# Cross-channel attention, 16 batches: X and G loaded a second time, and turned by 32x32 transposes on VectorE instead of on TensorE

## The reference

```python
def xca(q, k, v):
    attn = softmax(einsum('bhni,bhnj->bhij', q, k) * scale, axis=-1)
    return einsum('bhnd,bhde->bhne', v, attn)
res_p2r = xca(heads(rgb, wq_rgb), heads(geo, wk_point), heads(geo, wv_point)) @ proj_p2r.T
res_r2p = xca(heads(geo, wq_point), heads(rgb, wk_rgb), heads(rgb, wv_rgb)) @ proj_r2p.T
out = transpose(rgb + res_p2r) + transpose(geo + res_r2p)
```

## Time and profile before

| | |
|---|---|
| median of the runs | 145.45 us (145.23, 145.67, 145.45) |
| profiled execution, span of the trace | 144.7 us |
| TensorE busy | 135.4 us, 94% |
| VectorE busy | 99.1 us, 68% |
| ScalarE busy | 92.6 us, 64% |
| GpSimd busy | 2.0 us, 1% |
| DMA | 25.80 MB, 178 GB/s over the span |

### The profile page before, as it was taken

One profiled execution on the slowest core, in us unless ns is written; L12 is line 12 of the kernel. 1 busy time (PEld: TensorE's weight loads), 2 busy tenths in 40 slices (PEclk: granted clock), 3 DMA queues, 4 the chain that ended last, 5 costly groups with the idle time before them and its releaser, 6 DMA issues. The chain is left out here.

```text
span 144.7 us, 3130 instructions
## 1 busy us (share of the span) xinstructions
PE 135.4 (94%) x968; PEld 123.4 (85%) x968; DVE 99.1 (68%) x245; ACT 92.6 (64%) x207; POOL 2.0 (1%) x11
## 2 busy tenths in 40 slices
PE   7599889999999999999999999999999999997871
PEld 7399778999999998999999998989999998986560
DVE  0125797678686977777786878777785969777740
ACT  3125948675766767785876767686867677582821
POOL 5000000000000000000000000000000000000000
PEclk9959999999999999999999999999999999999998
DMA  4999243431919467482828475583927730303033
GB/s 132 246 418 417 96 140 150 147 147 31 348 61 248 191 183 249 142 289 60 296 86 263 172 239 196 165 270 89 310 53 245 317 147 0 145 0 150 2 147 145
DMA packets 7642, 25.80 MB, mean 178 GB/s; under 512 B 849, under 2 KB 977, under 8 KB 7633
## 3 DMA queue, kind: packets, MB, share of 16 engines
q1 hardware_dynamic: 7632, 25.69, 52.2%
HBM read 17.30 MB, written 8.39 MB: 178 GB/s over the span
## 5 line engine op out<-in xcount | busy, mean ns | idle before, releaser
L383 DVE COPY gt<-gt_ps 128x512 f32<-128x512 f32 x32 | 22.1, 691 | 18.1 <-PE gt_ps L228 18.1
L238 PE MATMUL gu_ps<-gt,xt 128*128 128x128 f32 x256 | 34.5, 281 | 0.0
L238 PEld LDWEIGHTS gu_ps<-gt,xt 128*128 128x128 f32 x256 | 33.2, 198 | 1.2
L372 ACT COPY out_sb<-out_ps 128x512 f32<-128x512 f32 x32 | 17.7, 587 | 18.0 <-DMA out_dram<-out_sb 11.0
L387 DVE TENSOR_TENSOR x_lo<-x_raw,x_hi 128x1024 fp32r<-128x1024 f32 x16 | 19.6, 1226 | 4.1 <-ACT x_hi L327 4.1
L318 ACT COPY xt<-xt_ps 128x512 f32<-128x512 f32 x32 | 18.9, 589 | 5.0 <-PE xt_ps L228 4.9
L354 ACT ACTIVATE expd<-scores,min_neg 128x128 f32<-128x128 f32 x32 | 12.6, 395 | 12.8 <-DVE min_neg L427 12.8
L228 PE MATMUL xt_ps<-ident,x_raw 128*128 128x128 f32 x128 | 19.3, 273 | 1.1 <-DMA x_raw<-in_x_dram 1.1
L228 PE MATMUL gt_ps<-ident,g_raw 128*128 128x128 f32 x128 | 19.8, 278 | 0.6 <-DMA g_raw<-in_ctx_dram 0.6
L387 DVE TENSOR_TENSOR g_lo<-g_raw,g_hi 128x1024 fp32r<-128x1024 f32 x16 | 19.5, 1216 | 0.0
L228 PEld LDWEIGHTS xt_ps<-ident,x_raw 128*128 128x128 f32 x128 | 15.4, 142 | 3.2 <-DMA x_raw<-in_x_dram 1.3
(11 more groups left out here) (51 smaller groups left out, 193.1 us busy)
## 6 DMA issues: line engine op xcount, KB each, us to landing
x_raw<-in_x_dram SPq DMA_DIRECT2D x15, 512.0 KB, 3.5
g_raw<-in_ctx_dram SPq DMA_DIRECT2D x15, 512.0 KB, 5.3
out_dram<-out_sb SPq DMA_DIRECT2D x15, 512.0 KB, 5.9
x_raw<-in_x_dram SPq DMA_DIRECT2D x2, 256.0 KB, 3.8
g_raw<-in_ctx_dram SPq DMA_DIRECT2D x2, 256.0 KB, 4.4
out_dram<-out_sb SPq DMA_DIRECT2D x2, 256.0 KB, 2.0
w_sb<-in_weights_dram SPq DMA_DIRECT2D x1, 384.0 KB, 7.1
w_sb<-in_weights_dram SPq DMA_DIRECT2D x1, 128.0 KB, 5.0
```

The source lines that it names most:

```text
L238: last = nc.tensor.matmul(gram_ps, xt[:, cols], gt[:, cols], start=(t == 0), stop=(t == TILES - 1))
L372: nc.scalar.copy(out_sb[:, slot % OUT_SLOTS, cols], out_ps[:, cols]).then_inc(half_copied, 1)
L383: nc.vector.tensor_copy(gt[:, cols], gt_ps[:, cols]).then_inc(gt_copied, 1)
```

## The change

- TensorE's 256 blocks turned against the identity are gone, with the 64 PSUM copies behind them. The PSUM that they took holds separate banks for gram, u/v, scores, exponentials, y and T.
- X and G are each loaded twice: once as before (`load_plain`, raw blocks for the split and the output), and once by `load_turned` into `xz` and `gz`. A "quad" is 32 partitions. The load of quad q brings pixels 256q to 256q+255 of all 128 channels to partitions 32q to 32q+31: channel 32a+k goes to partition 32q+k, column block a. That is one DMA per quad and tensor, of 1 KB rows: 128 rows for batches 0 and 1, 256 rows for a pair of batches after them. The quads go in the order 0, 2, 1, 3, all from SyncE. Two pairs of batches are held.
- VectorE turns 32x32 blocks with its own transpose (`turn_half`), four instructions of 128x512 in a step, from SBUF to SBUF. The pixels end up in another order within the sum, the same for X and G.
- The low parts of X and G (128x1024 each) move from VectorE to GpSimd, and wait there for the output stage of four batches before.
- The stages are one step deeper: VectorE turns batch i while TensorE makes gram i-1, small i-2, last i-3. T's matmuls are at the end of the small stage. ScalarE copies the second output half in the next step, and splits X of a batch before the gram's high part.
- The exponentials and the T sum stay in PSUM, the product with the reciprocal is one instruction instead of two, the output has four slots, and 56 warm-up matmuls stand in place of 24.
- The separate versions of the last steps (u/v copied by VectorE, T's high part made there) are gone, and the loops are written out.

```diff
-WARM = 24
+WARM = 56
-OUT_SLOTS = 2
+OUT_SLOTS = 4
+        def load_turned(eng, src, dst, done, first, count, quads):
+            pair, at = first // 2 % PAIRS, first % 2
+            for q in quads:
+                into = dst[q * QUAD:(q + 1) * QUAD, pair, at:at + count, :]
+                eng.dma_start(into.rearrange("p e (a m) -> p (e a) m", a=QUADS),
+                              src[q][:, QUADS * first:QUADS * (first + count), :]).then_inc(done, 16)
...
+            for b in range(B):
+                split_lo(b, x_raw, x_hi, x_lo, x_hi_ready)
+                split_lo(b, g_raw, g_hi, g_lo, g_hi_ready)
...
+            load_turned(sp, x_turn, xz, xz_first, 0, 1, (0, 2, 1, 3))
+            load_turned(sp, g_turn, gz, gz_first, 0, 1, (0, 2, 1, 3))
             sp.dma_start(w_sb[:, WQR:WKR + 1, :], weights[:, WQR:WKR + 1, :]).then_inc(wu_loaded, 16)
+            load_turned(sp, x_turn, xz, xz_loaded[0], 1, 1, (0, 2, 1, 3))
+            load_turned(sp, g_turn, gz, gz_loaded[0], 1, 1, (0, 2, 1, 3))
+            load_plain(0)
             sp.dma_start(w_sb[:, WKP:, :], weights[:, WKP:, :]).then_inc(w_loaded, 16)
+            load_turned(sp, x_turn, xz, xz_loaded[1], 2, 2, (0, 2, 1, 3))
+            load_turned(sp, g_turn, gz, gz_loaded[1], 2, 2, (0, 2, 1, 3))
+            for b in range(1, SLOTS):
+                load_plain(b)
+            for i in range(2, B + 4):
+                if i % 2 == 0 and i + 2 < B:
+                    sp.wait_ge(xt_turned, 2 * i)
+                    sp.wait_ge(gt_turned, 2 * i)
+                    load_turned(sp, x_turn, xz, xz_loaded[(i + 2) // 2 % PAIRS], i + 2, 2, (0, 2, 1, 3))
+                    load_turned(sp, g_turn, gz, gz_loaded[(i + 2) // 2 % PAIRS], i + 2, 2, (0, 2, 1, 3))
+                if 0 <= i - 4 < B - 1:
+                    store(i - 4)
+                if i >= 3 and i + 1 < B:
+                    sp.wait_ge(lo_ready, 2 * (i - 3) + 2)
+                    load_plain(i + 1)
...
+                if out_on:
+                    evacuate(e, 1)
...
+                if gram_on:
+                    split_hi(g, x_raw, x_loaded, x_hi, x_hi_ready)
...
+                if last_on:
+                    evacuate(l, 0)
                 if gram_on:
+                    act.wait_ge(gram_done, g + 1)
...
                     nc.scalar.copy(gram_hi[:, :], gram_ps).then_inc(gram_hi_ready, 1)
+                    split_hi(g, g_raw, g_loaded, g_hi, g_hi_ready)
...
+                blocks = src[:, pair, b % 2, :].rearrange("p (a j i) -> p j a i", a=QUADS, i=QUAD)
+                first = half * TILES // 2
                 cols = slice(half * HALF, (half + 1) * HALF)
+                nc.vector.transpose(dst[:, b % 2, cols].rearrange("p (j a k) -> p j a k", a=QUADS, k=QUAD),
+                                    blocks[:, first:first + TILES // 2, :, :]).then_inc(turned, 1)
```

More of the change, by code:

```diff
@@ L187, in _ @@
[L187 to L191, removed]
+                sp.dma_start(out[b], out_sb[:, b % OUT_SLOTS, :]).then_inc(out_stored[b % OUT_SLOTS], 16)
@@ L215, in _, with gram_half @@
                 nc.tensor.matmul(out_ps[:, 0:P], warm[:, :], warm[:, :], start=True, stop=True)
[L216 to L225, removed]
+            def gram_half(b, half):
+                pe.wait_ge(xt_turned, 2 * b + 1 + half)
+                pe.wait_ge(gt_turned, 2 * b + 1 + half)
+                if half == 0 and b >= 1:
+                    pe.wait_ge(gram_lo_ready, b)
@@ L226, in turn @@
                 for t in range(half * TILES // 2, (half + 1) * TILES // 2):
                     cols = slice(t * TILE, (t + 1) * TILE)
[L228 to L238, removed]
+                    last = nc.tensor.matmul(gram_ps, xt[:, b % 2, cols], gt[:, b % 2, cols], start=(t == 0),
+                                            stop=(t == TILES - 1))
@@ L239, in gram_half, with last_parts @@
                 if half == 1:
                     last.then_inc(gram_done, 1)
-            def last_half(b, slot, half, b_min):
+            def last_parts(b, half, first, end):
+                slot = b % SLOTS
                 cols = slice(half * HALF, (half + 1) * HALF)
-                if b_min >= 1:
-                    pe.wait_ge(half_copied, 2 * b - 1 + half)
                 parts = [(t_hi, 0, x_hi), (t_hi, 0, x_lo), (t_hi, 1, g_hi), (t_hi, 1, g_lo), (t_lo, 0, x_hi), (t_lo, 1, g_hi)]
-                for n, (w, which, moving) in enumerate(parts):
+                if first == 0 and b >= 1:
+                    pe.wait_ge(half_copied, 2 * (b - 1) + 1 + half)
+                for n in range(first, end):
+                    w, which, moving = parts[n]
@@ L248, in last_half @@
                     if half == 0 and n == 4:
                         pe.wait_ge(t_lo_ready, b + 1)
[L250 to L259, removed]
+                    last = nc.tensor.matmul(out_ps[:, cols], w[:, which, :], moving[:, slot, cols], start=(n == 0),
+                                            stop=(n == len(parts) - 1))
@@ L260, in step @@
+                if end == len(parts):
+                    last.then_inc(half_done, 1)
+            for i in range(1, B + 3):
+                g, s, l = i - 1, i - 2, i - 3
+                gram_on, small_on, last_on = g < B, 0 <= s < B, 0 <= l < B
                 if small_on:
-                    pe.wait_ge(gram_lo_ready, i)
-                    if i_min == 1:
+                    pe.wait_ge(gram_lo_ready, s + 1)
+                    if s == 0:
                         pe.wait_ge(wu_lo_ready, 1)
@@ L306, in step @@
                 if last_on:
-                    last_half(i - 2, before, 1, i_min - 2)
-            steps(pe, step, 0, B + 1)
+                    last_parts(l, 1, 2, 6)
+                if small_on:
+                    pe.wait_ge(y_copied, s + 1)
+                    if s >= 1:
+                        pe.wait_ge(t_lo_ready, s)
+                    nc.tensor.matmul(t_ps[:, 0:P], y_sb[:, 1, :], w_sb[:, PR, :], start=True, stop=True)
+                    nc.tensor.matmul(t_ps[:, P:2 * P], y_sb[:, 0, :], w_sb[:, PP, :], start=True,
+                                     stop=True).then_inc(t_done, 1)
@@ L374, in _, with split_hi, evacuate @@
-            steps(act, step, 0, B + 1)
+            def split_hi(b, raw, loaded, hi, hi_ready):
+                slot = b % SLOTS
+                act.wait_ge(loaded[slot], 16 * (b // SLOTS) + 16)
+                if b >= SLOTS:
+                    act.wait_ge(half_done, 2 * (b - SLOTS) + 2)
+                nc.scalar.copy(hi[:, slot, :], raw[:, slot, :]).then_inc(hi_ready, 1)
+            def evacuate(b, half):
+                act.wait_ge(half_done, 2 * b + 1 + half)
+                if half == 0 and b >= OUT_SLOTS:
+                    act.wait_ge(out_stored[b % OUT_SLOTS], 16 * (b // OUT_SLOTS))
+                cols = slice(half * HALF, (half + 1) * HALF)
+                nc.scalar.copy(out_sb[:, b % OUT_SLOTS, cols], out_ps[:, cols]).then_inc(half_copied, 1)
@@ new lines, in turn_half @@
+            def turn_half(b, half, src, first_loaded, loaded, dst, turned):
+                pair = b // 2 % PAIRS
+                if b == 0:
+                    dve.wait_ge(first_loaded, 64)
+                elif b == 1:
+                    dve.wait_ge(loaded[0], 64)
+                else:
+                    dve.wait_ge(loaded[pair], 64 * (b // 2 // PAIRS) + 64)
+                if b >= 2:
+                    dve.wait_ge(gram_done, b - 1)
+                blocks = src[:, pair, b % 2, :].rearrange("p (a j i) -> p j a i", a=QUADS, i=QUAD)
+                first = half * TILES // 2
+                cols = slice(half * HALF, (half + 1) * HALF)
+                nc.vector.transpose(dst[:, b % 2, cols].rearrange("p (j a k) -> p j a k", a=QUADS, k=QUAD),
+                                    blocks[:, first:first + TILES // 2, :, :]).then_inc(turned, 1)
```

302 lines of the change are left out of this document (122 added, 180 removed).

## The result

The changed kernel takes **164.94 us** (median of 4 runs, 161.84 to 170.02), the kernel before beside it 145.56 (4 runs, 145.23 to 146.64): ratio 1.1164, 95% interval 1.1078 to 1.1251. It was forecast at 139 us, 6 us quicker than before; it is 19 us slower by the medians, 17 by the ratio, so the sign was wrong, and the median lies 0.94 us above the end of the range.

What follows compares the result with a forecast made beforehand. DMA was taken as the bound: 16.78 MB turned at 280 GB/s (59.9 us) and 18.35 MB at 415 (44.2), from 2.2 us, reach 106.3; with 5.1, 12.9, 6.6 and 7.7 after, 138.6, plus 0.75: 139 us, range 121 to 164.

Steps and rivals of the forecast that it cites:

- Bounds of a turned load's rate: DMA of the second, turned loads: between 187 and 417 GB/s, taken as 280, so 16.78 MB take 59.9 us.
- half-rate rival: DMA: turned loads run at half the full rate, 208 GB/s, taking 80.7 us, 160 us in all; chance 0.36.
- X: Time when the last turned pair (batches 14, 15) has landed in the DMA queue, put at 106.3 us.
- tail: After the last turned pair lands: VectorE's turning 5.1 us, two full steps 12.9, then 6.6 and 7.7 us.
- VectorE's turning among its other work: First term after the last turned pair has landed: VectorE turns it within its step's work, 5.1 us.
- I take the queue as never empty: DMA queue until the last turned pair lands: always filled, since each load is issued two steps ahead of use.
- TensorE, 6.43 us a step: TensorE's step without turning falls from 8.09 by 1.66 to 6.43 us, 26.6 us over 16 steps.
- VectorE, 0.69 us a transpose: Four 512-column transposes a step on VectorE at 0.69 us, 2.8 us, together 5.1 us a step.
- the rival of double cost: VectorE's transposes take 1.38 us each, a step 7.9 us, 145 us in all, no change; VectorE-bound chance 0.06.
- GpSimd, 4.8 us a step, hidden: Two low parts of 1024 columns a step on GpSimd, 3.2 to 6.4 us, middle 4.8, needed two steps later.
- SyncE, 2.3 to 2.7 us of issue a step: SyncE issues 7 DMAs a step in 2.3 to 2.7 us, 4.1 if 256 rows cost double; it fits.
- TensorE-bound rival: Turned loads run as fast as plain ones, TensorE stays the bound at 6.43 us a step, 124 us; chance 0.18.

Runs made afterwards that it cites:

- a2: The changed kernel with each second-load DMA writing all 128 partitions instead of a quad, same bytes and 1 KB rows, rearrangement left out: 136.57 us, ratio 0.9396.
- a3: The changed kernel with the second load in 4 KB rows, still 32 partitions per DMA, pixel rearrangement left out: 160.93 us, ratio 1.1009.
- a4: The changed kernel with the second load only for batches 0 to 3, later batches turning old blocks: 139.04 us, ratio 0.9578.
- d2: a4 with batches 2 and 3 loaded turned singly, plain 1 between, and ScalarE's gram high part before X's split: 132.70 us, ratio 0.9089.
- c1: Half of the changed kernel's change: only G loaded twice and turned on VectorE, X turned by TensorE from every eighth column: 146.70 us, ratio 0.996.
- c2: c1 with batches 2 and 3 loaded turned singly, gram's high part before X's split, VectorE's first transpose behind masked scores: 143.80 us, ratio 0.9798.

## Why the prediction was wrong

- **The failed step: "Bounds of a turned load's rate: 187 GB/s below, 417 above. I take 280."** It measured 207 to 231 in the pair of steps shown, about 215, half of the full queue's 415. The choice went by the middle one of the earlier trace rows, and all three of those are windows of loads onto all 128 partitions. a2 and a3 show that of the two new things the target carried the price, and that was the one for which there was no row. The half-rate rival had this step right and, at 208 GB/s, the price (160 us); I gave it 0.36.
- **The sum with the measured rate.** X becomes 2.2 + 16.78 / 0.215 + 44.2 = 124.4 us; the last turned G was waited for until 127.66. With the tail of 32.3 that makes 156.7 us of span, with 0.75 it is 157.5. A pair of steps becomes 2.1 MB / 0.215 + 3.15 MB / 0.415 = 9.8 + 7.6 = 17.4 us, measured 16.8 to 17.9.
- **The other 7 us.** 3.3 are in X: by the slices of the page's GB/s row 36.2 MB had gone through by then, 1.1 MB more than the 35.1 of my sum, which is 2.6 us at 415 GB/s. The order of issue was as in my count (13 plain pairs and 8 stores in front of the last turned pair). The store and the plain loads issued behind it, from 118.39 on, are where the extra bytes can come from; no row tells them apart. 3.9 are in the tail, 36.2 instead of 32.3: "VectorE's turning among its other work" was not last, the plain X queued behind the turned loads was, until 131.20, and TensorE, idle from 129.3 to 133.8, went on at a granted clock of 0.50 (1.2 GHz) in the windows from 134 to 138.
- **"I take the queue as never empty"** was right: DMA share 1.00 to 1.17 in the windows from 34 to 130 us. **DMA-bound** was right as well; the sign hung on the rate, as a2 shows (0.9396 with the faster loads).
- **TensorE, 6.43 us a step:** 6.28 in a4 and in d2. Right, within 0.15.
- **VectorE, 0.69 us a transpose:** 0.70. Right; the rival of double cost is out in the changed kernel.
- **GpSimd, 4.8 us a step, hidden:** 2 x 2.37 = 4.74, and its waits are for ScalarE. Right. The figure in the Trainium skill, GPSIMD Engine Reference, section Performance versus the Vector engine, had given an estimated 2.25 us; the trace agrees within 6%.
- **SyncE, 2.3 to 2.7 us of issue a step:** eight turned loads alone took 11.2 us in two steps. In the first microseconds eight of 128 KB took 3.7 (0.74 to 4.45), so the time is the full queue's, not the issue's. But it holds up the plain loads behind it, and I had priced that at nothing.
- **ScalarE: "a late plain load holds up the gram's split".** The place was right, the victim another: the split of X stands in front of the exponentials, so y waits (27.5 us), and the gram's split after it.
- **The start** was in my X but not in the TensorE-bound rival: with no second load after the first four batches, a4 took 139 where that rival said 124. So even a second load that cost nothing from then on would bring 6 us in this form (a4), with a better start 13 (d2), not 21.

## What to carry to other kernels

Before a load is cut into pieces that each fill a few partitions, price it at the share of the partitions it reaches, and look for a form that writes all 128: here the same bytes in the same rows cost 26 us more on 32 partitions at a time. When a new load has two new properties and the trace has rows for one, do not take the rate from those rows; give the chances by the property that has none. Where one queue carries both, count what the slow loads do to the others behind them, at the start above all.

## What had not been expected

- A transpose on VectorE from every eighth column takes 1.17 to 1.19 us for 128x512 (c1, c2) where groups of 32 neighbours take 0.70. So half the transposes are 37.3 us in c1, where all of them are 45.0 in the changed kernel. In c2:

```profile
L395 DVE STREAM_TRANSPOSE gt<-gz 128x512 f32<-128x512 f32 x32 | 38.1, 1190 | 8.6 <-DMA gz<-in_ctx_dram 8.6
```

- The full queue's rate depends on row length far less than the earlier trace rows suggested: 347 to 372 GB/s with 1 KB rows on all partitions (a2), 415 with 4 KB.
- The changed kernel's runs scatter by 5% (161.84 to 170.02), those of the kernel before by 1%. Where a late DMA left TensorE idle, the granted clock was 0.50 or little more in a stretch behind it, as at 116 to 118 us after 3.1 us of waiting. That this makes the scatter was not tested, and it is not all of it: the mean granted clocks of the four runs, 0.863 to 0.881, lie within 2%, and the one of 170.02 us had 0.866, the one of 165.73 us 0.863.
